# Attention scores in 64-row tiles with four masked key copies, four rotating PSUM banks, and the values stage moved to the middle of the step

## The chip, the cores and the metric

The kernel runs on one core of a Trainium2 chip. The metric is the device time of one execution in microseconds (us), the median over several runs.

## The reference

x has the shape [16, 64, 64, 64] (images n, rows a, columns b, channels d). Four blocks follow each other, each added to x after a layer normalization:

1. Attention over the 16 images, for each pixel (a, b) by itself: q, k, v and a gate from 64 channels, 8 heads of 16 channels, softmax over the 16 images, o times the gate, then a projection back to 64 channels.
2. A mixture of experts on each pixel: router logits for 8 experts, the best two by softmax, a 64 x 64 expert each.
3. An expansion to 128 channels; a running average along the row axis a of the gating half, its sigmoid times the other half, and a contraction to 64 channels.
4. A selection: for each of 32 slots and each image a softmax over the 4096 pixels, the 8 best pixels pooled, a small network, and the result added back to those pixels.

```python
att = jnp.einsum('iabhc,jabhc->ijabh', q, k) * (1.0 / np.sqrt(C))
att = jax.nn.softmax(att, axis=1)
o = jnp.einsum('ijabh,jabhc->iabhc', att, v) * g
```

## The kernel before

The work of blocks 1 to 3 is cut into 128 items, each half a column of the images: 512 tokens in 4 tiles of 128 (32 rows a by 16 images). A software pipeline works on up to nine items at a time. One **slot** is a pass through the body `step(i, q)` on each engine, q being 0 or 1; an operation with lag L works in slot n on item n - L (the table `LAG`: att_t, q, k, gate and v have lag 1, scores 2, values and att_out 3, route and y0 to y3 4, conv_t and expand 5, scan_out 7, pick_t and pick 8). Buffers that live from one lag to another come in pairs. Each engine's order is written out by hand in `step`, the five engines meet through counting semaphores, and `at(i, q, lag)` is the count that stands for "the item with this lag in this slot". Block 4 follows after all slots, in a phase of its own.

TensorE order before: att_t (transposes), scores, q, values, ffn_t, v, scan_out, gate, k, att_out, pick_t, route, pick, conv_t, y0, expand, y1, y2, y3. The first slots and the last ones leave out the parts whose item doesn't exist.

**Scores.** The 8 heads lie along 128 partitions, 16 to a head. To keep heads apart, ScalarE writes 8 copies of k (lines 470 to 474), each with all rows but those of one head set to zero. 32 matmuls in tiles of 128 rows by 32 columns (line 640), 128 columns streamed each, fill one PSUM bank. VectorE takes the maxima (817) and subtracts them (819), ScalarE takes the exponential (507), VectorE sums (852), takes the reciprocal (854) and multiplies by an odd/even head mask to own_den (857); GpSimd forms probs (414), and VectorE transposes them in 32 x 32 blocks to probsT (918). One slot later the values (line 658: 64 matmuls of 32 x 32 tiles) fill the four o_bank banks, and VectorE multiplies them by the gate (839, output ogT; "the gated read" below). Each fp32 matmul appears as two instructions in the trace.

**The gate.** gT is one of the buffers in a pair. ScalarE writes it with a Tanh, at lag 1, and first waits until the gated read of the item that had this buffer, lag 3 in the same slot, is over:

```python
act.wait_ge(filled["gate"], at(i, q, 1))
wait(act, s_og, at(i, q, 3))
s.activation(gT[z1][:], bk("gate")[:], ACT.Tanh, bias=bg_col[:],
             scale=0.5).then_inc(drained["gate"], 1)
```

**PSUM.** Two `shared` banks are used in turn by the operations of `TURNS`; `s_bank` has two banks and `o_bank` four, and six further operations borrow banks of these (`BORROWED`). Before TensorE fills a bank it waits until its last user there is drained, that is, read by ScalarE or VectorE.

ScalarE order before: zT, rounding of ffn, qT, rounding of att, tT, the copy of v, exp, the Tanh of gT, masked copies 0 and 1, rounding of conv, lT (the drain of pick_t), copies 2 and 3, picks, cT, lge, copies 4 and 5, four parts of expand, copy 6, gT plus one, in slots with q = 0 the Tanh of the scan (ema_t), copy 7. VectorE order before: statistics of att, expert sum `mixed` (811), maxima and subtraction of the scores, x2 and statistics of conv, gated read, x3 add (848), sums to own_den, scan gating in slots with q = 1, x1 add (868) and statistics of ffn, statistics of pick, the route's logits (880) and the choice of two experts, yg of y0 and y1 (912), transpose of probs, in slots with q = 0 the scan, yg of y2 and y3 (932), and the gating for q = 0. SyncE issues three groups of eight DMAs a slot: the next x, the normalized x3 and x3.

Of the kernel before, what the change touches and what calls it, by code (L numbers as in the profile page):

```python
# [45 lines left out]
def build(nc, x, ln_w, ln_b, Wq, Wk, Wv, Wg, bg, Wo, bo, router_w, router_b, expert_w, expert_b,  # L46
# [24 lines left out]
    with ExitStack() as ctx:  # L71
# [12 lines left out]
        shared = [ctx.enter_context(nc.psum_tensor(f"shared{i}", [P, 512], F32)) for i in range(2)]  # L84
        s_bank = ctx.enter_context(nc.psum_tensor("s_bank", [P, 2, 512], F32))
# [3 lines left out]
        with ExitStack() as cols:  # L89
# [12 lines left out]
            b_k = cb("b_k", [P, H])  # L102
# [19 lines left out]
            odd_even = cb("odd_even", [P, 2])  # L122
            decay = cb("decay", [P, 8, A])
# [18 lines left out]
            kT = cb("kT", [P, H, QTOK])  # L142
# [26 lines left out]

            filled = {k: sem(f"filled_{k}") for k in TURNS + list(BORROWED)}  # L170
            drained = {k: sem(f"drained_{k}") for k in TURNS + list(BORROWED)}
# [12 lines left out]
            s_sums, s_v = sem("exp_summed"), sem("values_biased")  # L184
# [7 lines left out]
            N_DVE_SETUP = 11  # L192
# [32 lines left out]
            def bank_of(q, name):  # L225
                if name in BORROWED:
                    whose, bank = BORROWED[name]
                    return {"o": o_bank, "s": s_bank}[whose][:, bank]
                return shared[(len(TURNS) * q + TURNS.index(name)) % 2][:]

            def last_drained(i, q, name):

                pos = len(TURNS) * q + TURNS.index(name)
                for back in range(pos - 2, pos - 6 * len(TURNS), -2):
                    slots_back, turn = divmod(back, len(TURNS))
                    prev = TURNS[turn]
                    if not isinstance(i, int) or 0 <= 2 * i + slots_back - LAG[prev] < HALVES:
                        return drained[prev], at(i, slots_back, LAG[prev])
# [96 lines left out]
            def _(pool):  # L335
# [54 lines left out]
                def step(i, q):  # L390
# [9 lines left out]
                    if runs(i, q, 5):  # L400
                        normalize("conv", x2[par(q, 5)], 1.0, 1e-6, i, q, 5, "conv_t")
                    if runs(i, q, 1):
# [5 lines left out]
                    if runs(i, q, 5):  # L408
                        second_part("conv", i, q, 5)
                    if runs(i, q, 2):  # L410

                        pool.wait_ge(s_rden, at(i, q, 2))
                        wait(pool, s_probsT, at(i, q, 3))
                        g.tensor_tensor(probs[:], weights[:].unsqueeze(2).broadcast_to([P, 32, 2, 16]),  # L414
                                        own_den[:].unsqueeze(3).broadcast_to([P, 32, 2, 16]), ALU.mult).then_inc(s_probs, 1)
# [22 lines left out]
            def _(act):  # L438
# [27 lines left out]
                def step(i, q):  # L466
# [33 lines left out]
                    if runs(i, q, 1):  # L500
                        act.wait_ge(filled["v"], at(i, q, 1))

                        wait(act, s_o, at(i, q, 3))
                        s.copy(v_sb[z1][:].rearrange("p t c -> p (t c)"), bk("v")[:]).then_inc(drained["v"], 1)  # L504
# [3 lines left out]
                    if runs(i, q, 1):  # L508
# [8 lines left out]
                        masked_keys(range(0, 2))  # L517
# [7 lines left out]
                    if runs(i, q, 1):  # L525
                        masked_keys(range(2, 4))
# [15 lines left out]
                    if runs(i, q, 1):  # L542
                        masked_keys(range(4, 6))
# [13 lines left out]
                    if runs(i, q, 1):  # L557
                        masked_keys(range(6, 7))

# [5 lines left out]
                    if runs(i, q, 1):  # L565
                        masked_keys(range(7, H)).then_inc(drained["k"], 1)

# [620 lines left out]
```

## Time and profile before

| | before |
|---|---|
| median of 3 runs | 3134.15 us (3130.02 to 3141.3) |
| the profiled execution | 3123.18 us, span 3121.5 us |
| TensorE matmul busy | 2647.5 us (85%) |
| VectorE busy | 2551.6 us (82%) |
| GpSimd busy | 2161.0 us (69%) |
| ScalarE busy | 2005.1 us (64%) |
| mean granted TensorE clock | 0.839 |

The span runs from the first to the last instruction of the profiled execution. Busy shares are means over the span, of which the last 270 us or so belong to block 4. PE is TensorE, PEld its weight loads, DVE VectorE, ACT ScalarE, POOL GpSimd, SP SyncE. A granted clock of 1.00 is 2.4 GHz and one of 0.50 is 1.2 GHz.

### The profile page before, as it was taken

The page shows a single profiled execution, that of the slowest core. Times are in us where ns is not written, and L with a number is a line of the kernel's source. Part 1 is how long each engine was busy: PE and PEld are TensorE (multiplying, and loading weights), DVE is VectorE, ACT ScalarE, POOL GpSimd, SP SyncE. Part 2 cuts the span into 40 slices and gives each one's busy share as a digit, 9 for nine tenths or more (in the row PEclk, how much of TensorE's full clock was granted, in tenths as well). Part 3 has the DMA queues.
Part 4 walks back from the last instruction along what each step waited for, and adds up shares of the span by engine and source line. Part 5 has one row for each costly group of instructions (what it writes and reads, how often), then busy time and mean ns, then how long its engine had stood idle before and what let it go on. Part 6 is the DMA issues. An engine that isn't in the chain of part 4 may idle for free. (4 is left out here: it accounts for less than half of the span.)

```text
span 3121.5 us, 108500 instructions
## 1 busy us (share of the span) xinstructions
PE 2647.5 (85%) x37071; PEld 1969.9 (63%) x37071; DVE 2551.6 (82%) x9002; ACT 2005.1 (64%) x3590; POOL 2161.0 (69%) x2963
## 2 busy tenths in 40 slices
PE   2898898888888888898898898888988988896697
PEld 2666666666666656666666666666666666664586
DVE  2788889888888898888888888888889888885604
ACT  2666767766676676776776766677667676762600
POOL 2677777877777777777787877778777777863000
PEclk9788988887888888888887987889889788885858
DMA  0011101111011010110101111011010010101828
GB/s 17 9 20 18 19 17 19 19 18 19 17 19 18 18 19 17 19 19 18 19 17 18 19 18 19 17 19 19 18 19 18 17 19 18 19 15 19 269 96 337
DMA packets 263153, 106.67 MB, mean 34 GB/s; under 512 B 250257, under 2 KB 254900, under 8 KB 258997
## 3 DMA queue, kind: packets, MB, share of 16 engines
q1 hardware_dynamic: 260933, 93.16, 12.9%
q10 hardware_dynamic: 2160, 12.68, 1.0%
q8 instruction: 40, 0.66, 0.1%
q14 instruction: 20, 0.16, 0.0%
HBM read 55.31 MB, written 50.33 MB: 34 GB/s over the span
## 5 line engine op out<-in xcount | busy, mean ns | idle before, releaser
L472 ACT ACTIVATE kT<-s_bank,b_k,block_of 128x512 f32<-128x512 f32 x1024 | 748.8, 771 | 3.6 <-PE s_bank L609 0.3
L640 PE MATMUL s_bank<-kT,qT 128*32 128x128 f32 x8192 | 396.1, 372 | 187.3 <-issue 187.3
L640 PEld LDWEIGHTS s_bank<-kT,qT 128*32 128x32 f32 x8192 | 349.5, 152 | 226.8 <-issue 224.7
L489 ACT ACTIVATE qT<-shared,b_qkg 128x256 f32<-128x256 f32 x256 | 107.5, 471 | 412.0 <-PE shared L609 412.0
L811 DVE TENSOR_REDUCE mixed<-yg 128x256 f32<-128x2048 f32 x128 | 288.5, 2254 | 0.2
L687 PEld LDWEIGHTS o_bank<-w_o,ogT 128*128 128x128 f32 x2048 | 247.9, 193 | 23.7 <-DVE ogT L839 14.8
L414 POOL TENSOR_TENSOR probs<-weights,own_den 128x1024 f32<-128x1024 f32 x128 | 252.7, 1975 | 1.8 <-DVE own_den L857 1.8
L687 PE MATMUL o_bank<-w_o,ogT 128*128 128x64 f32 x2048 | 246.9, 274 | 4.3 <-DVE ogT L839 3.9
L387 POOL TENSOR_TENSOR split_ffn<-norm_ffn,split_ffn 128x256 fp32r<-128x256 f32 x128 | 93.6, 731 | 215.1 <-ACT split_ffn L464 215.1
L658 PEld LDWEIGHTS o_bank<-probsT,v_sb 32*32 32x32 f32 x16384 | 170.2, 107 | 63.7 <-issue 58.1
L658 PE MATMUL o_bank<-probsT,v_sb 32*32 32x64 f32 x16384 | 196.5, 234 | 1.5 <-DVE yg L932 1.5
L387 POOL TENSOR_TENSOR split_att<-norm_att,split_att 128x256 fp32r<-128x256 f32 x128 | 94.0, 735 | 147.4 <-ACT split_att L464 147.4
L622 PE MATMUL shared<-bias,ones 3*128 3x512 bf16 x256 | 109.3, 427 | 98.3 <-ACT picks L532 52.2
L555 ACT ACTIVATE gpre<-shared,bgate_col 64x256 f32<-64x256 f32 x256 | 181.4, 709 | 13.3 <-PE shared L721 10.3
L593 PE MATMUL shared<-ident,split_att 128*128 128x128 f32 x512 | 111.6, 357 | 69.3 <-ACT prim L555 47.9
L377 POOL TENSOR_TENSOR rstd_ffn<-rstd_ffn,minus_half 128x4 f32<-128x4 f32 x128 | 160.1, 1251 | 10.7
L406 POOL TENSOR_TENSOR v_sb<-v_sb,bv_rows 128x512 f32<-128x512 f32 x128 | 163.1, 1274 | 3.0 <-ACT v_sb L504 3.0
L839 DVE TENSOR_TENSOR ogT<-o_bank,gT 128x512 f32<-128x512 f32 x256 | 163.2, 679 | 1.5 <-PE o_bank L658 1.2
L918 DVE STREAM_TRANSPOSE probsT<-probs 128x1024 f32<-128x1024 f32 x128 | 157.9, 1234 | 2.0 <-POOL probs L414 2.0
L593 PEld LDWEIGHTS shared<-ident,split_att 128*128 128x128 f32 x512 | 78.4, 182 | 123.3 <-issue 68.2
L800 DVE SCALAR_TENSOR_TENSOR gated<-ema_t,prim 64x256 f32<-64x256 f32 x256 | 150.3, 587 | 6.8 <-ACT ema_t L564 1.1
L677 PE MATMUL shared<-w_con,gated 128*128 128x64 f32 x1024 | 141.8, 283 | 7.9 <-DVE gated L800 5.8
(204 smaller groups left out, 7648.6 us busy)
## 6 DMA issues: line engine op xcount, KB each, us to landing
x_in<-in_x SPq DMA_DIRECT2D x1024, 16.0 KB, 1.7
x_scratch<-x SPq DMA_DIRECT2D x1024, 16.0 KB, 1.4
normalized_x_scratch<-norm_pick SPq DMA_DIRECT2D x1024, 16.0 KB, 1.5
xa<-normalized_x_scratch SPq DMA_DIRECT2D x16, 1024.0 KB, 8.1
xb<-x_scratch ACTq DMA_DIRECT2D x8, 1024.0 KB, 10.3
out_x<-xa SPq DMA_DIRECT2D x16, 512.0 KB, 5.3
out_x<-xb SPq DMA_DIRECT2D x16, 512.0 KB, 6.9
xa<-x_scratch SPq DMA_DIRECT2D x4, 1024.0 KB, 6.5
```

Source lines behind the costliest of these rows:

```text
L377: ch.link(g.tensor_tensor(r[:, 1, :], r[:, 0, :], minus_half[:], ALU.pow))
L387: g.tensor_tensor(split[kind][z][:, :, 1, :], norm[kind][z][:], split[kind][z][:, :, 0, :].bitcast(F32), ALU.subtract).then_inc(s_split[ki ...
L406: g.tensor_tensor(v_sb[z][:], v_sb[z][:], bv_rows[:].unsqueeze(1).broadcast_to([P, QT, HC]), ALU.add).then_inc(s_v, 1)
L414: g.tensor_tensor(probs[:], weights[:].unsqueeze(2).broadcast_to([P, 32, 2, 16]), own_den[:].unsqueeze(3).broadcast_to([P, 32, 2, 16]), AL ...
L472: ins = s.activation(kT[:, h, :], bk("k")[:], ACT.Identity, bias=b_k[:, h:h + 1], scale=block_of[:, h:h + 1])
L555: ins = s.activation(dst, src, ACT.Identity, bias=bias[r0:r0 + D], scale=scale)
L593: ins = t_.transpose(bank_of(q, name)[:, t * P:(t + 1) * P], split[kind][par(q, lag)][:, t].rearrange("p k d -> p (k d)").bitcast(F32), id ...
L640: ins = t_.matmul(s_bank[g * 32:(g + 1) * 32, 0, t * P:(t + 1) * P], qT[z][:, c, tok:tok + 32], kT[:, :, tok + c * N:tok + (c + 1) * N], s ...
L658: ins = t_.matmul(o_bank[k * 32:(k + 1) * 32, g, t * 64:(t + 1) * 64], v_sb[z][g * 32:(g + 1) * 32, t, k * 32:(k + 1) * 32], pT[g * 32:(g ...
L687: ins = t_.matmul(bk("att_out")[:, t * D:(t + 1) * D], ogT[:, h, tile(t)], w_o2[:, h, :], start=(h == 0), stop=(h == 1))
L811: v.tensor_reduce(mixed[:], yg[:], AX.X, ALU.add).then_inc(s_mixed, 1)
L839: ins = v.tensor_tensor(by_group(ogT[:, h, :]), o, by_group(gT[z][:]), ALU.mult)
```

## The change

- **Scores.** Head m and head m + 4 share one masked copy of k (`quarter` has ones on both), so four copies are written instead of eight. Each score matmul is split in two, on rows 0 to 63 and 64 to 127 (index u), with 64 streamed columns each; the halves go to banks 0 and 1 of `o_bank`: 64 matmuls instead of 32. VectorE reads both banks. The head order in weights, probs and probsT changes with it.
- **PSUM.** `s_bank` and `BORROWED` go. There are four `shared` banks, and the table `BANK` gives each of 17 operations its bank. `o_bank` is used by scores and values in turn, so scores wait for the last gated read, and values wait for the subtraction of this slot's scores.
- **TensorE order.** Values move from behind q to behind pick_t; v moves from behind ffn_t to behind the values; pick_t is now ahead of both; att_out moves from behind k to behind expand. v has bank 3 after pick_t, route bank 0 after scan_out.
- **VectorE order.** The gated read moves behind x3, the sums, the reciprocal, the gating for q = 1 and the statistics of pick. The x1 add and the statistics of ffn move behind yg of y0 and y1.
- **ScalarE order.** The copy of v moves behind lT; the masked copies are 0 after the Tanh of gT, 1 after the copy of v, 2 and 3 after lge. No copy is left behind ema_t.
- **GpSimd.** own_den is computed here, ahead of probs, and the addition of v's bias comes after both.

```diff
-TURNS = ["att_t", "q", "ffn_t", "v", "scan_out", "gate", "pick", "conv_t", "y0", "expand", "y3"]
-BORROWED = {"y2": ("o", 0), "att_out": ("o", 1), "pick_t": ("o", 2), "route": ("o", 3),
-            "y1": ("s", 0), "k": ("s", 1)}
+TURNS = ["att_t", "q", "ffn_t", "scan_out", "gate", "k", "pick_t", "v", "route", "pick", "conv_t", "y0", "expand",
+         "att_out", "y1", "y2", "y3"]
+BANK = {"att_t": 0, "q": 1, "ffn_t": 2, "v": 3, "scan_out": 0, "gate": 1, "k": 2, "pick_t": 3, "route": 0, "pick": 1,
+        "conv_t": 3, "y0": 1, "expand": 3, "att_out": 0, "y1": 1, "y2": 2, "y3": 3}
...
 # GpSimd
+                    if runs(i, q, 5):
+                        second_part("conv", i, q, 5)
+                    if runs(i, q, 2):
+                        pool.wait_ge(s_rden, at(i, q, 2))
+                        g.tensor_tensor(own_den[:], ssum[:].unsqueeze(2).broadcast_to([P, 32, 2]),
+                                        odd_even[:].unsqueeze(1).broadcast_to([P, 32, 2]), ALU.mult).then_inc(s_own, 1)
+                        pool.wait_ge(s_own, at(i, q, 2))
...
 # ScalarE
-                                               scale=block_of[:, h:h + 1])
+                                               scale=quarter[:, h:h + 1])
...
-                        masked_keys(range(0, 2))
+                        masked_keys(range(0, 1))
...
+                        act.wait_ge(filled["v"], at(i, q, 1))
+                        wait(act, s_o, at(i, q, 3))
+                        s.copy(v_sb[z1][:].rearrange("p t c -> p (t c)"), bk("v")[:]).then_inc(drained["v"], 1)
+                    if runs(i, q, 1):
+                        masked_keys(range(1, 2))
...
-                        masked_keys(range(4, 6))
+                        masked_keys(range(2, 4)).then_inc(drained["k"], 1)
...
 # TensorE
-                        wait_apart(pe, (drained["k"], at(i, q, 2)), (drained["q"], at(i, q, 2)), (s_sub, at(i, q, 3)),
-                                   (drained["y1"], at(i, q, 5)))
+                        wait_apart(pe, (drained["k"], at(i, q, 2)), (drained["q"], at(i, q, 2)), (s_og, at(i, q, 4)))
                         for t in range(QT):
                             for c in range(2):
                                 for g in range(4):
-                                    tok = t * P + g * 32
-                                    ins = t_.matmul(s_bank[g * 32:(g + 1) * 32, 0, t * P:(t + 1) * P],
-                                                    qT[z][:, c, tok:tok + 32], kT[:, :, tok + c * N:tok + (c + 1) * N],
-                                                    start=(c == 0), stop=(c == 1), tile_position=(0, g * 32))
+                                    for u in range(2):
+                                        tok, rows = t * P + g * 32, slice(u * D, (u + 1) * D)
+                                        ins = t_.matmul(o_bank[g * 32:(g + 1) * 32, u, t * D:(t + 1) * D],
+                                                        qT[z][rows, c, tok:tok + 32],
+                                                        kT[rows, :, tok + c * N:tok + (c + 1) * N],
+                                                        start=(c == 0), stop=(c == 1), tile_position=(u * D, g * 32))
...
-                        wait_apart(pe, (s_norm["pick"], at(i, q, 8)))
+                        wait_apart(pe, (s_norm["pick"], at(i, q, 8)), last_drained(i, q, "pick_t"))
...
+                    if runs(i, q, 3):
+                        z = par(q, 3)
+                        wait_apart(pe, (s_probsT, at(i, q, 3)), (s_v, at(i, q, 3)), (s_og, at(i, q, 4)),
+                                   (s_sub, at(i, q, 2) if runs(i, q, 2) else HALVES))
...
+                    if runs(i, q, 1):
+                        bank_free(pe, i, q, "v")
...
+                        bank_free(pe, i, q, "route")
...
 # VectorE
+                    if runs(i, q, 2):
+                        dve.wait_ge(s_exp, at(i, q, 2))
+                        v.tensor_reduce(ssum[:], weights[:], AX.X, ALU.add).then_inc(s_sums, 1)
+                        dve.wait_ge(s_sums, at(i, q, 2))
+                        v.reciprocal(ssum[:], ssum[:]).then_inc(s_rden, 1)
+                    if q == 1 and runs(i, 1, 6):
+                        gate_primary()
+                    if runs(i, q, 7):
+                        dve.wait_ge(drained["scan_out"], at(i, q, 7))
+                        stats("pick", x3[par(q, 7)], i, q, 7)
                     if runs(i, q, 3):
                         z = par(q, 3)
                         dve.wait_ge(s_o, at(i, q, 3))
```

## Rows read from the trace of the kernel before

**Rows 1.** Line 811 by source: duration min/median/max, first and last start.

```profile
L811 DVE TENSOR_REDUCE mixed<-yg x128: 2249/2253/2286, 110.2 to 2852.3; 128x256 f32<-128x2048 f32 x128
```

**Rows 2.** One stretch: PE, PEld, DVE, ACT, POOL busy, PEclk, DMA share, GB/s.

```profile
300.00:2700.00 2400.00, 2110.23 (x30639) 1542.85 (x30638) 2120.67 (x7714) 1687.34 (x3053) 1871.42 (x2553) 0.86 0.10 18
```

**Rows 3.** The waits: who waited for whom, us in total, times, longest.

```profile
PE s_bank L640 <- issue: 187.3, 116, 5.2
...
DVE x L848 <- PE shared L677: 71.1, 88, 2.1
...
DVE smax L817 <- PE s_bank L640: 61.4, 53, 3.9
...
DVE x L868 <- PE o_bank L687: 33.0, 66, 3.1
DVE yg L912 <- PE s_bank L624: 32.8, 31, 1.7
...
ACT gT L512 <- DVE ogT L839: 22.8, 25, 2.0
```

**Rows 4.** The costliest groups on the page: the masked key copies.

```profile
L472 ACT ACTIVATE kT<-s_bank,b_k,block_of 128x512 f32<-128x512 f32 x1024 | 748.8, 771 | 3.6 <-PE s_bank L609 0.3
```

**Rows 5.** Timeline, scores and values of three slots: start, us, what.

```profile
59.48 3.64 PE L640 MATMUL s_bank<-kT,qT 128*32 128x128 f32 x64 [5.17 <-issue]
...
1519.11 1.47 PE L658 MATMUL o_bank<-probsT,v_sb 32*32 32x64 f32 x128
...
1558.04 1.95 PE L640 MATMUL s_bank<-kT,qT 128*32 128x128 f32 x64 [1.47 <-issue]
```

**Rows 6.** Timeline, VectorE from one slot to the next.

```profile
1501.89 0.42 DVE L848 TENSOR_TENSOR x<-shared,x_bc 128x256 f32<-128x256 f32 x1 [1.00 <-PE shared L677]
...
1503.33 0.49 DVE L857 TENSOR_TENSOR own_den<-ssum,odd_even 128x64 f32<-128x64 f32 x1
...
1506.07 0.57 DVE L777 BATCH_NORM_STATS2 bn_pick<-x 128x6 f32<-128x64 f32 x4
...
1519.32 0.69 DVE L819 TENSOR_TENSOR weights<-s_bank,smax 128x512 f32<-128x512 f32 x1
...
1521.43 1.29 DVE L839 TENSOR_TENSOR ogT<-o_bank,gT 128x512 f32<-128x512 f32 x2
```

**Rows 7.** Timeline, ScalarE and VectorE in the middle of a slot.

```profile
1502.22 0.69 ACT L512 ACTIVATE gT<-shared,bg_col 128x512 f32<-128x512 f32 x1 [0.29 <-PE shared L609]
...
1504.13 0.41 ACT L464 CAST split_conv<-norm_conv 128x256 fp32r<-128x256 f32 x1
...
1504.86 0.58 ACT L524 COPY lT<-o_bank 64x512 f32<-64x512 f32 x1 [0.31 <-PE o_bank L694]
...
1507.03 0.16 DVE L880 TENSOR_TENSOR lg<-o_bank,rb_rows 128x32 f32<-128x32 f32 x1
...
1509.62 0.69 DVE L912 TENSOR_TENSOR yg<-shared,gates 128x512 f32<-128x512 f32 x1
```

**Rows 8.** Timeline, TensorE: v, att_out, route, y0's start, y1's end.

```profile
1521.01 1.06 PE L670 MATMUL shared<-w_scaled,zT 128*128 128x128 f32 x8
...
1523.85 1.89 PE L687 MATMUL o_bank<-w_o,ogT 128*128 128x64 f32 x16
...
1526.02 0.96 PE L700 MATMUL o_bank<-w_router,tT 128*128 128x8 f32 x8
...
1528.63 0.38 PE L622 MATMUL shared<-bias,ones 3*128 3x512 bf16 x1 [0.44 <-ACT picks L532]
...
1530.73 0.40 PE L624 MATMUL s_bank<-w_expert_lo,tT 128*128 128x512 f32 x1
```

**Rows 9.** Timeline, TensorE near the start of the run: v twice.

```profile
48.45 2.08 PE L670 MATMUL shared<-w_scaled,zT 128*128 128x128 f32 x8 [0.93 <-ACT qT L489]
...
65.17 1.16 PE L670 MATMUL shared<-w_scaled,zT 128*128 128x128 f32 x8 [0.93 <-ACT qT L489]
```

More of the change, by code:

```diff
@@ L83, in build @@
         picks = sb("picks", [P, NG, TOK])
[L84 to L85 removed]
+        shared = [ctx.enter_context(nc.psum_tensor(f"shared{i}", [P, 512], F32)) for i in range(4)]
         o_bank = ctx.enter_context(nc.psum_tensor("o_bank", [P, 4, 512], F32))
@@ L682, in step @@
                         project("k", 1)
-                    if runs(i, q, 3):
-                        pe.wait_ge(s_og, at(i, q, 3))
-                        for t in range(QT):
-                            for h in range(2):
-                                ins = t_.matmul(bk("att_out")[:, t * D:(t + 1) * D], ogT[:, h, tile(t)], w_o2[:, h, :],
-                                                start=(h == 0), stop=(h == 1))
-                        ins.then_inc(filled["att_out"], 1)
                     if runs(i, q, 8):
-                        wait_apart(pe, (s_norm["pick"], at(i, q, 8)))
+                        wait_apart(pe, (s_norm["pick"], at(i, q, 8)), last_drained(i, q, "pick_t"))
                         for t in range(QT):
@@ L721, in step @@
                         t_.matmul(bk("expand")[:], w_expand_lo[:], cT[:], start=False, stop=True).then_inc(filled["expand"], 1)
+                    if runs(i, q, 3):
+                        bank_free(pe, i, q, "att_out")
+                        pe.wait_ge(s_og, at(i, q, 3))
+                        for t in range(QT):
+                            for h in range(2):
+                                ins = t_.matmul(bk("att_out")[:, t * D:(t + 1) * D], ogT[:, h, tile(t)], w_o2[:, h, :],
+                                                start=(h == 0), stop=(h == 1))
+                        ins.then_inc(filled["att_out"], 1)
                     if runs(i, q, 4):
@@ L829, in step @@
                         stats("conv", x2[z], i, q, 5)
+                    if runs(i, q, 7):
+                        z = par(q, 7)
+                        dve.wait_ge(filled["scan_out"], at(i, q, 7))
+                        dve.wait_ge(s_x2bc, at(i, q, 7))
+                        wait(dve, s_x3_store[z], (column(i, q, 9) + 1) * 128)
+                        wait(dve, s_norm["pick"], at(i, q, 9))
+                        v.tensor_tensor(x3[z][:], tok(bk("scan_out")), x2_bc[z][:], ALU.add).then_inc(drained["scan_out"], 1)
+                    if runs(i, q, 2):
[5 more added lines that the diff above has]
+                        gate_primary()
+                    if runs(i, q, 7):
+                        dve.wait_ge(drained["scan_out"], at(i, q, 7))
+                        stats("pick", x3[par(q, 7)], i, q, 7)
                     if runs(i, q, 3):
@@ L913, in step @@
                                             gates[:, t, :].unsqueeze(1).broadcast_to([P, D, NE]), ALU.mult).then_inc(drained[y], 1)
+                    if runs(i, q, 3):
+                        z = par(q, 3)
+                        dve.wait_ge(filled["att_out"], at(i, q, 3))
+                        dve.wait_ge(s_bo, at(i, q, 3))
+                        wait(dve, s_norm["ffn"], at(i, q, 5))
+                        wait(dve, s_x2, at(i, q, 5))
+                        v.tensor_tensor(x1[z][:], tok(bk("att_out")), x_bo[z][:], ALU.add).then_inc(drained["att_out"], 1)
+                        dve.wait_ge(drained["att_out"], at(i, q, 3))
+                        stats("ffn", x1[z], i, q, 3)
                     if runs(i, q, 2):
@@ L937, in _ @@
                 slots(dve, step)
-        banks = [s[:] for s in shared] + [s_bank[:, k] for k in range(2)] + [o_bank[:, k] for k in range(4)]
+        banks = [s[:] for s in shared] + [o_bank[:, k] for k in range(4)]
         with ExitStack() as imgs:
```

126 lines of the change are left out of this document (37 added, 89 removed).

## The prediction

> **What bounds the kernel now.** I read the views in this order: the page, for busy shares; the stretches of time, for one steady window; one line with its first and last start, for the length of a slot; the waits; then the timeline of two neighbouring slots. The chain that ended last is no help: it covers only the closing phase, which the change leaves alone.
>
> The line that sums the experts runs once a slot, 128 times, from 110.2 to 2852.3 us [rows 1], so a slot is 2742.1 / 127 = 21.59 us. In the window 300 to 2700 us [rows 2] that makes per slot: VectorE busy 2120.67 / 2400 x 21.59 = 19.1 us, TensorE 19.0, GpSimd 16.8, ScalarE 15.2. VectorE is idle 2.5 us a slot. The waits [rows 3] put 71.1 + 61.4 + 33.0 + 32.8 = 198.3 us of that, 1.55 us a slot, down to TensorE results; the other 0.95 us are joins between its own dependent instructions and small waits. TensorE's largest single stall is 187.3 us in front of the scores [rows 3], 1.5 us a slot: it waits there through registers, so the row says "issue", and in every second slot ScalarE's last masked copy, queued behind the Tanh of the scan, is what arrives late. So no engine is saturated; VectorE and TensorE are both within 2.6 us of the slot, and the rest is order. What the change does to the order therefore decides.
>
> **The parts that look like gains.** (a) Four masked copies instead of eight: the copy takes 0.77 us [rows 4], so 3.1 us of ScalarE a slot go, and none stands behind the Tanh of the scan any more; the 1.5 us stall before the scores can go. (b) The scores: 64 instructions of 128 columns took 1.95 us at the full clock and 3.64 at half [rows 5]. After, 128 instructions of 64 columns. Bounds: the values stage already issues 128 instructions of 64 columns in 1.47 us [rows 5], and no less; no overlap of the two row halves leaves today's 1.95 to 3.64. I take the values' price, it is the same count and width: 0.5 to 2 us less TensorE. The Trainium skill ("TensorEngine Tiling (Array Packing)", Theoretical Speedup) allows up to 2x for a contraction of 64; by that the full clock stage would be about 1.0 us, an estimate that no row here shows. (c) The product with the odd/even mask, 0.49 us in the slot shown [rows 6], leaves VectorE. On GpSimd I bound it between 0.2 us and its cost on VectorE twice over, 1.0; I take 0.3. GpSimd has 4.8 us free a slot and its product is read only at the transpose, some 9 us later in the new order, so it is hidden; without that cover it would cost its own time. (d) The reads of the scores from two banks have as many elements as before: nothing. The setup gains one tiny reduction before the loop: nothing. No DMA is added; the three groups of eight on SyncE keep their order and wait for events that merely move.
>
> VectorE's own floor becomes 19.1 - 0.5 + 0.95 = 19.5 us a slot.
>
> **The part that costs.** Follow one wait that the change does not touch. ScalarE's Tanh of the gate (line 512) writes a buffer that the gated read (line 839) of the same slot still needs, two slots' work being in flight in a pair of buffers, and so waits for that read. Today the read comes early: it ended at 1522.7 [rows 6], and the Tanh still waited for it 25 times, 22.8 us in all [rows 3]. The change moves the values behind the scores' reading, and on VectorE the gated read behind the x3 add, the sums, the reciprocal and the statistics of pick. In the slot shown 2.7 us passed from the end of the subtraction (1520.01) to the end of the gated read (1522.72) [rows 6]; now x3 to reciprocal (1501.89 to 1503.33, 1.44 us) and the statistics (1506.07 to 1507.03, 0.96) [rows 6, 7] come in between: 5.1 us, 6 where a slot has the scan's gating there too.
>
> Queued behind the waiting Tanh on ScalarE are the first masked copy, the rounding of conv, the copy lT and then the copy of v. TensorE's v now sits in bank 3 behind pick_t, so it needs lT; and route, which VectorE needs next, is queued behind v. VectorE, having ended the gated read, goes straight to the route's logits. So it waits for a chain that starts only when it finishes:
>
> 1. ScalarE, Tanh start to end of the conv rounding: 1502.22 to 1504.54 = 2.32 us with two masked copies [rows 7], one less 0.77 [rows 4] = 1.55; lT 0.58 [rows 7]; with handoffs 2.2 us.
> 2. TensorE, v 1.06 and route 0.96 [rows 8]: 2.0 us at full clock. First hole: 4.2 us.
> 3. VectorE then works from the logits to the end of y0's product, 1507.03 to 1510.31 = 3.3 us [rows 7].
> 4. Next it wants y1. TensorE from v's start: v 1.06; from the start of route to the end of y1, with pick, conv_t, y0 and expand between them, 1526.02 to 1531.13 = 5.11; and att_out, now ahead of y1, 1.89 [rows 8]: 8.1 us. Second hole: 8.1 - 2.0 - 3.3 = 2.8 us.
>
> The holes make 2.2 + 8.1 - 3.3 = 7.0 us, none of it beside other VectorE work. The other inputs, followed in the same way (exp, scan_out, the transposed probabilities), come in time, since all engines but VectorE gain slack from the longer slot. Slot at full clock: 19.5 + 7.0 = 26.5 us.
>
> **The clock.** TensorE ends the values 1.5 us after the subtraction and then stands for 5.1 - 1.5 + 2.2 = 5.8 us, in every slot. After an idle stretch of 5.17 us the scores took 3.64 us and v, 5.7 us after the restart, 1.16 again [rows 5, 9], so the 1.2 GHz level stood for most of the first 5 us. The page "TensorE: Matmul & The Clock Gate" (Part 1) of the Trainium skill calls the throttled level the default, which activity releases. By that, and the trace agrees, v starts slow in each slot. At half clock v took 2.08 (+1.0) [rows 9]; route with as many weight loads gets likewise +1.0, and conv_t with half as many +0.5 (an estimate). The chain is then 8.1 + 2.5 = 10.6 and the holes 2.2 + 10.6 - 3.3 = 9.5: a slot of 29.0 us, 7.4 more than now.
>
> **The sum.** The holes need lags 1, 3, 4 and 8 together: slots 8 to 127, 120 of them. The execution profiled took 3123.2 us (span 3121.5 and 1.7 around it). 3123 + 120 x 7.4 = 4011. My step 4 adds durations that overlap by about 0.1 at each seam, 0.3 in all and 36 us over the run, so I take 3980. The median of runs lies 11 us above the profiled one: 3990.
>
> **The rivals.**
> - *Full clock.* The stop doesn't lower the clock, or it recovers at once: 26.5 a slot, 3123 + 120 x 4.9 = 3711. For it: v was fast again within 5.7 us of a restart. Against: such stops now come every slot. 0.2.
> - *Only the first hole.* y1 is there when VectorE asks, and the clock is full: 19.5 + 4.2 = 23.7, 3123 + 120 x 2.1 = 3375. It needs 2.8 us of TensorE work to vanish. 0.1.
> - *Half clock all along.* The rest doubles like v, y0 to y1 from 1528.63 to 1531.13 (2.50) and att_out (1.89) [rows 8]: +4.4, a slot of 33.4, 3123 + 120 x 11.8 = 4539. 0.12.
> - *Faster.* The Tanh isn't held by this slot's gated read (its count being met by the last one's), so the chain runs under VectorE's work, and the stall before the scores and half the copies are saved: 19.5 a slot, 3123 - 128 x 2.1 = 2854. It decides if the Tanh starts at least 4.2 us before the gated read ends. Against it stands the row with 25 waits. 0.07.
> - *No change.* Gain and holes cancel: 21.6 = 19.5 + 2.1, half of the first hole. 0.03.
>
> **How the numbers follow.** The slow-start case has 0.48 and gives the forecast, 3990. Differences under 0.3% (9 us) cannot be told from none. Slower 0.90, same 0.03, faster 0.07. The range from the single first hole to near the all-slow case, 3380 to 4450, leaves about 0.15 outside.
>
> **What would show it.** Right: the Tanh waiting on the gated read in nearly every slot, some 4 us each, 500 us in all; VectorE's logits (line 880 now) waiting on TensorE's route 4 to 6 us a slot and its yg product on y1 about 2.5; TensorE idle 5 to 6 us before v, released by lT; v near 2 us; the scores stage near 1.5 and its stall gone; mean clock under 0.8. Wrong: the Tanh starting before the gated read, or logits without a wait. The forecast fails low if the clock stays up, high if it never recovers.

## The result and the profile after

| | before | after |
|---|---|---|
| median | 3137.73 us (3130.02 to 3146.6, 4 runs) | 4466.19 us (4464.67 to 4555.35, 4 runs) |
| the profiled execution | 3123.18 us | 4555.35 us, span 4553.6 us |
| TensorE matmul busy | 2647.5 us (85%) | 3589.7 us (79%) |
| VectorE busy | 2551.6 us (82%) | 2430.6 us (53%) |
| mean granted TensorE clock | 0.839 | 0.594 |

The ratio is 1.423 (95% interval 1.419 to 1.4272): slower by 1328 us. The forecast was 3990 and its range ended at 4450, so the time lies 16 us above the range. The profiled execution of the changed kernel was its slowest of four, 2% over the median, at a clock of 0.594 where the others had about 0.66; its rows show the pattern, and where a size matters the median is used.

The line of the expert sum by source (columns as in [rows 1]), and a steady stretch (as [rows 2]):

```profile
L802 DVE TENSOR_REDUCE mixed<-yg x128: 2250/2253/2287, 124.4 to 4293.7; 128x256 f32<-128x2048 f32 x128
```

```profile
300.00:4200.00 3900.00, 3143.73 (x39867) 2289.43 (x39870) 2127.65 (x8031) 1477.63 (x2751) 1983.15 (x2815) 0.58 0.07 12
```

A slot is (4293.7 - 124.4) / 127 = 32.83 us here. What lies outside the 127 slots is 4555.35 - 4169.3 = 386 us, so at the median a slot is (4466.19 - 386) / 127 = 32.1 us, against 21.59. In a slot of 32.83 VectorE works 2127.65 / 3900 x 32.83 = 17.9 us and TensorE 26.5: VectorE now stands for 14.9 us a slot, not 2.5. The waits of the changed kernel (columns as in [rows 3]) say for what:

```profile
POOL x_bo L423 <- DVE x L899: 1212.9, 126, 9.8
DVE lg L858 <- PE shared L681: 718.2, 125, 5.9
DVE yg L890 <- PE shared L611: 631.5, 128, 5.1
ACT gT L510 <- DVE ogT L851: 610.4, 126, 5.7
...
PE shared L674 <- ACT lT L522: 455.9, 121, 4.3
...
DVE bn_att L768 <- DMA x_in<-in_x: 248.6, 128, 16.9
...
DVE sel L874 <- ACT lge L544: 108.1, 125, 2.3
DVE ogT L851 <- PE o_bank L666: 98.4, 95, 2.8
```

The wait for the load had this row before:

```profile
DVE bn_att L777 <- DMA x_in<-in_x: 34.0, 11, 14.5
```

The Tanh waited for the gated read 25 times before [rows 3] and now does so in 126 slots, 4.8 us each. Read the VectorE rows as a list of holes, each total over its count: the logits 5.7 us a slot, yg 4.9, the load of the next x 1.9, sel 0.9, the gated read 1.0 where it waits (0.8 over all slots). Together 14.2 of the 14.9 us.

One slot in the timeline, all engines:

```profile
1500.90 3.86 SPq L313 DMA_DIRECT2D x_in<-in_x  x8
...
1503.02 2.05 PE L627 MATMUL o_bank<-kT,qT 64*32 64x64 f32 x128
...
1506.07 0.61 DVE L768 BATCH_NORM_STATS2 bn_att<-x_in 128x6 f32<-128x64 f32 x4 [0.40 <-DMA x_in<-in_x]
...
1516.09 1.29 DVE L851 TENSOR_TENSOR ogT<-o_bank,gT 128x512 f32<-128x512 f32 x2 [0.38 <-PE o_bank L666]
1517.48 0.69 ACT L510 ACTIVATE gT<-shared,bg_col 128x512 f32<-128x512 f32 x1 [4.91 <-DVE ogT L851]
...
1519.65 2.08 PE L674 MATMUL shared<-w_scaled,zT 128*128 128x128 f32 x8 [3.69 <-ACT lT L522]
1519.88 0.29 POOL L407 TENSOR_TENSOR own_den<-ssum,odd_even 128x64 f32<-128x64 f32 x1
...
1521.52 1.71 PE L681 MATMUL shared<-w_router,tT 128*128 128x8 f32 x8
...
1523.27 0.19 DVE L858 TENSOR_TENSOR lg<-shared,rb_rows 128x32 f32<-128x32 f32 x1 [5.89 <-PE shared L681]
...
1527.20 3.51 PE L708 MATMUL shared<-w_o,ogT 128*128 128x64 f32 x16
...
1532.44 0.69 DVE L890 TENSOR_TENSOR yg<-shared,gates 128x512 f32<-128x512 f32 x1 [5.05 <-PE shared L611]
1533.05 0.42 DVE L899 TENSOR_TENSOR x<-shared,x_bo 128x256 f32<-128x256 f32 x1
...
1533.54 0.73 POOL L423 TENSOR_TENSOR x_bo<-x_in,bo_rows 128x256 f32<-128x256 f32 x1 [9.84 <-DVE x L899]
```

From 1516.09 to 1523.27 the reader sees the forecast chain link by link: gated read, Tanh, v behind lT, route, logits. What the forecast did not have starts at the last two rows. The x1 add (L899) is now the end of the chain att_out, y1, yg; x_bo on GpSimd waits for it, the eight loads of the next x are issued after x_bo (in the slot ahead they began at 1500.90 and took 3.86 us to issue), and VectorE wants that x for the next statistics at 1506.07.

And the clock, in stretches of 2 us of the same slot (TensorE busy, then granted clock):

```profile
1516.00:1518.00 2.00, 0.00 (x0) 1.00 0.19 30
...
1520.00:1522.00 2.00, 2.00 (x11) 0.50 0.00 0
...
1528.00:1530.00 2.00, 2.00 (x11) 0.50 0.00 0
...
1534.00:1536.00 2.00, 2.00 (x7) 0.50 0.05 10
```

The granted level is 2.4 GHz (1.00) where TensorE stands, and 1.2 GHz (0.50) through the 16 us of work from v to y3. The forecast had it last about 5. Not every slot is like this one. e3 below takes as long as the changed kernel's median and has the same order on TensorE; its trace has one such stretch at 0.50 as well, with v from 1519.16, and in the next slot, with v from 1552.57, the level comes back after 9 to 10 us of work:

```profile
1554.00:1556.00 2.00, 2.00 (x12) 0.50 0.16 25
...
1562.00:1564.00 2.00, 2.00 (x12) 1.00 0.00 0
```

### The profile page after: what moved, and what is told of

It is laid out like the page before. It is cut to its first block and busy times, and to the rows that moved or that the text cites. A ratio compares the mean times of both kernels' runs of the same rounds, so it can differ in the third digit from the quotient of the medians.

```text
span 4553.6 us, 124326 instructions
## 1 busy us (share of the span) xinstructions
PE 3589.7 (79%) x45263; PEld 2650.8 (58%) x45263; DVE 2430.6 (53%) x8875; ACT 1673.3 (37%) x3078; POOL 2170.3 (48%) x3091
## 5 line engine op out<-in xcount | busy, mean ns | idle before, releaser
L674 PE MATMUL shared<-w_scaled,zT 128*128 128x128 f32 x1024 | 263.5, 438 | 455.9 <-ACT lT L522 455.9
L674 PEld LDWEIGHTS shared<-w_scaled,zT 128*128 128x128 f32 x1024 | 226.6, 326 | 479.1 <-ACT lT L522 478.0
L708 PEld LDWEIGHTS shared<-w_o,ogT 128*128 128x128 f32 x2048 | 462.8, 330 | 25.3 <-issue 1.0
L708 PE MATMUL shared<-w_o,ogT 128*128 128x64 f32 x2048 | 445.3, 411 | 0.7 <-DVE ogT L851 0.7
L610 PE MATMUL shared<-w_expert_hi,tT 128*128 128x512 f32 x512 | 403.8, 789 | 0.0
L475 ACT ACTIVATE kT<-shared,b_k,quarter 128x512 f32<-128x512 f32 x512 | 383.1, 776 | 0.2 <-PE shared L603 0.2
L602 PE MATMUL shared<-zT,w_qkg_hi 128*128 128x512 f32 x384 | 285.9, 745 | 60.3 <-ACT tT L502 51.9
L611 PE MATMUL shared<-w_expert_lo,tT 128*128 128x512 f32 x512 | 319.0, 623 | 0.0
L627 PE MATMUL o_bank<-kT,qT 64*32 64x64 f32 x16384 | 257.7, 305 | 4.6 <-issue 4.6
L627 PEld LDWEIGHTS o_bank<-kT,qT 64*32 64x32 f32 x16384 | 229.5, 142 | 46.9 <-issue 46.9
```

The lines of the kernel that those rows point to most:

```text
L602: t_.matmul(bk(name)[:], w_qkg_hi[:, w, :], zT[z1][:], start=True, stop=False)
L610: t_.matmul(bk(y)[:], tT[z4][:, tile(t)], w_expert_hi[:], start=False, stop=False)
L611: t_.matmul(bk(y)[:], tT[z4][:, tile(t)], w_expert_lo[:], start=False, stop=True).then_inc(filled[y], 1)
L627: ins = t_.matmul(o_bank[g * 32:(g + 1) * 32, u, t * D:(t + 1) * D], qT[z][rows, c, tok:tok + 32], kT[rows, :, tok + c * N:tok + (c + 1) * N],
L674: ins = t_.matmul(bk("v")[:, tile(t)], zT[z1][:, tile(t)].bitcast(F32), w_scaled[:, 3, :])
L708: ins = t_.matmul(bk("att_out")[:, t * D:(t + 1) * D], ogT[:, h, tile(t)], w_o2[:, h, :], start=(h == 0), stop=(h == 1))
```

## The experiments

Each starts from the changed kernel unless the diff says otherwise. The ratio is against the kernel before on the same chip; slots are from the first and last start of the expert sum, over 127, in the profiled execution.

**e1, the Tanh freed.** It writes a buffer of its own; the step that adds one, later in the slot, waits for the gated read instead.

```diff
-    wait(act, s_og, at(i, q, 3))
-    s.activation(gT[z1][:], bk("gate")[:], ACT.Tanh, ...)
+    wait(act, s_gp1, at(i, q, 2))
+    s.activation(g_raw[:], bk("gate")[:], ACT.Tanh, ...)
...
-    s.activation(gT[z1][:], gT[z1][:], ACT.Identity, bias=one_col[:])
+    wait(act, s_og, at(i, q, 3))
+    s.activation(gT[z1][:], g_raw[:], ACT.Identity, bias=one_col[:])
```

> The changed kernel with one wait moved: the Tanh of the gate writes a buffer of its own, and the late add of one, which now carries the wait for the gated read, writes the pair buffer. Same instructions otherwise. Theory (order): the chain from the gated read over Tanh, masked copy, rounding, lT, v and route to the logits is what fills the slot; with the Tanh free it runs under VectorE's work, the wait of the logits falls from 5.9 us a slot to about nothing, TensorE no longer stands before v, the clock rises over 0.8, and the slot goes from 32 us to 22 to 24: 3150 to 3400 us. Rival (clock or tiles): the 64-row score tiles or the four banks keep TensorE slow by themselves; then the clock stays near 0.6 and the time above 3900 us.

Measured 3634.56 us (1.1523, 1.147 to 1.1575), slot 25.65. This gives back 832 of the 1328 us, more than any other single edit, and part of that is the clock, which rises from about 0.66 to 0.75. It still ends 235 us above the theory's band. VectorE's longest waits:

```profile
DVE yg L892 <- PE shared L613: 271.3, 128, 5.1
DVE bn_att L770 <- DMA x_in<-in_x: 243.3, 128, 17.2
DVE lg L860 <- PE shared L683: 172.0, 124, 3.0
```

The wait for x_in is as long as with the Tanh held: it has another cause.

**e2, the stand filled.** The Tanh stays held; TensorE multiplies constants, which nobody reads, before v.

```diff
+    bank_free(pe, i, q, "route")
+    for _ in range(16):
+        t_.matmul(bk("route")[:], w_expand_hi[:], w_expert_hi[:], start=True, stop=True)
```

> The changed kernel with 16 matmuls of 512 columns (weights times weights, result never read) put in TensorE's stand between values and v, in the bank that route overwrites. No work is left out. They take 3.4 us at full clock and 6.8 at half, within the stand of about 6 us. Theory: the lasting half clock comes from this stand and from the other one, and it doubles the chain; with it filled the clock rises over 0.8 and the slot goes to the full-clock sum of 26.5 us, 3700 us in all. Rival: the clock has little to do with it, or stays low for another reason; then 4466 us or more.

Measured 3911.08 (1.2461, 1.2426 to 1.2495), clock 0.843, slot 27.69. More work makes it 555 us shorter, though not down to the 3700 expected. att_out takes 1.89 us, its price at full clock:

```profile
1513.62 1.89 PE L711 MATMUL shared<-w_o,ogT 128*128 128x64 f32 x16
```

VectorE's longest waits, to be held against the forecast's slot at full clock:

```profile
DVE lg L861 <- PE shared L684: 541.3, 126, 5.2
DVE bn_att L771 <- DMA x_in<-in_x: 245.9, 128, 21.8
DVE yg L893 <- PE shared L611: 174.1, 128, 5.1
```

The logits wait 4.3 us (worked out: 4.2), yg 1.4 (2.8), and 1.9 for the load (none).

**e3, the gated read ahead of the x3 add on VectorE.**

> The changed kernel with only VectorE's order changed: the gated read goes back ahead of the x3 add, the values stay where the change put them. Theory: the chain starts earlier by the x3 add, the sums, the reciprocal, the gating and the statistics of pick (2.4 us, 3.3 in odd slots), which VectorE then does while the chain runs, so the holes shrink by up to 2.4 to 3.3 us a slot, less if VectorE waits for the values: 4050 to 4300 us. Rival (only the bank order matters): no change, 4466 us.

Measured 4467.66 (1.4231): no change, against the theory. VectorE's holes only move:

```profile
DVE yg L890 <- PE shared L611: 557.6, 128, 5.1
DVE ogT L832 <- PE o_bank L666: 432.4, 128, 6.7
DVE lg L858 <- PE shared L681: 388.5, 125, 3.7
```

The read waits for the values themselves, which stand behind pick_t in mid step. The time is the rival's, but its reason, the order of the banks, is not what the rows show. In the changed kernel VectorE's place for the read was therefore not what made it late; no run puts the values back at their old place.

**e4, the scores alone**: the kernel before with 64-row tiles and four copies, all else in its old order; k waits for the last subtraction, since the scores now fill both banks of `s_bank`.

> The kernel before with only the 64-row score tiles and the four masked copies; bank of scores half 1 is the one that k fills later, so k waits for the subtraction too. Order untouched. Theory: the score stage goes from 1.95 to 3.6 us to about 1.5 to 2, the stall of 1.5 us a slot ahead of it mostly goes, ScalarE loses 3.1 us a slot; the slot goes from 21.6 to about 20 to 20.5 us: 2900 to 3000 us. Rival: the tiles cost the clock or the two halves do not overlap; then 3130 us or more.

Measured 3098.56 (0.9879, 0.9851 to 0.9907): a gain of 38 us, smaller than expected; whether the tiles or the fewer copies give it was not separated. Two score stages in its timeline, at half and at full clock:

```profile
1500.42 2.06 PE L639 MATMUL s_bank<-kT,qT 64*32 64x64 f32 x128
...
1519.33 1.49 PE L639 MATMUL s_bank<-kT,qT 64*32 64x64 f32 x128
```

against 3.64 and 1.95 [rows 5]. The tiles do what the forecast said; VectorE, busy 2185.53 of 2400 us in this kernel, leaves little to gain.

**e5 and e6, att_out early**: between v and route, with the x1 add and the statistics of ffn ahead of the logits (route shares att_out's bank and so waits for the x1 add); e6 frees the Tanh too, as e1.

```diff
-         "pick_t", "v", "route", "pick", "conv_t", "y0", "expand", "att_out", "y1", ...
+         "pick_t", "v", "att_out", "route", "pick", "conv_t", "y0", "expand", "y1", ...
```

> The changed kernel with att_out moved back towards its old place: on TensorE between v and route (bank 0, so route waits for the x1 add), on VectorE the x1 add and the statistics of ffn ahead of the logits. The Tanh's wait stays. Theory (two chains): besides the chain over the Tanh there is a second, from the late att_out over the x1 add, x_bo, the normalization of pick and the next slot's normalization of ffn on GpSimd to ffn_t, scan_out, k and so the values; the two are nearly tied, so that undoing one alone gives some, 150 to 600 us: 3850 to 4300. Rival (Tanh chain alone bounds): that chain gets longer by att_out's 1.9 to 3.5 us ahead of route, though the second hole goes with it: 4400 us or more.

Measured 4240.39 (1.3484, 1.3426 to 1.3542), slot 30.37, within the expected band: 226 us come back. The wait for x_in falls from 248.6 to 37.5 us in all; x1's own wait for att_out, 935.5, takes the place of those on the logits and on yg.

> Both undone: att_out early as in the run before, and the Tanh writes a buffer of its own so that only the late add of one waits for the gated read. Theory (two chains, nothing else large): near the kernel before, slot of 20.5 to 23 us, 3000 to 3300 us, clock over 0.8. Rival (the four-bank table or the values' place hold it up by themselves): over 3450 us, with waits of TensorE on a bank's drain or of VectorE on the values on top of the list.

Measured 3726.01 (1.1851, 1.1788 to 1.1914), slower than e1: a miss. With the Tanh free, att_out in front of route and x1 in front of the logits make VectorE wait 453.4 us in all for att_out, more than the load's wait that goes.

**e7, e1 with x_bo last on GpSimd.**

> The kernel with the staged Tanh (3635 us) and one GpSimd instruction moved: the x_bo add, which waits for the x1 add and so for att_out, goes from ahead of the normalization of pick to the end of the step. att_out stays late. Theory: GpSimd's standing before x_bo (731 us there) pushes the normalizations of pick and ffn and with them ffn_t; with the add last, normalization of pick and x2_bc run during that stand, 3.4 us of GpSimd work leave the second chain: 3250 to 3500 us. Rival (that stand is harmless, the clock or the bank order sets the time): 3600 us or more.

Measured 4046.26 (1.2857), 412 us slower than e1, where a gain was expected. The load's wait stays (252.1 us in all, 243.3 in e1), and those for y1 (552.8) and for the logits (318) about double, at a clock of 0.63 where e1 had 0.75. Moving x_bo behind the rest of GpSimd's work does not make the load come earlier; by which path it costs 412 us was not followed.

**e8 and e12, more on top of e4**: own_den on GpSimd (e8), and the freed Tanh as well (e12).

> The kernel before with the 64-row score tiles and four copies, and also the product with the odd/even mask on GpSimd right before probs. Theory: 0.5 us a slot less on VectorE, which is the busiest engine there (91% in the steady part), 0.3 more on GpSimd, which has slack: 3030 to 3080 us against 3099 without. Rival: VectorE is not the bound; no change, 3090 to 3110.

> The kernel before with the score tiles, four copies, the mask product on GpSimd (3094 us) and the staged Tanh. There the Tanh waits for the gated read 130 us in 72 slots. Theory: that wait goes, ScalarE gains up to 1 us in those slots, of which some reaches the end: 3050 to 3090 us. Rival: ScalarE is off the path there, no change within 0.3%.

Measured 3093.53 (0.9851, 0.9804 to 0.9898) and 3110.02 (0.9896, 0.987 to 0.9922). The mask product's move is worth no more than can be measured, and freeing the Tanh is worth nothing in the old order, where the gated read is early. Both missed what was expected; e8 fits its rival, no change, and e12 lies 0.5% above e8, their intervals overlapping. e8 is the fastest of all kernels run, 5 us ahead of e4.

**e9 and e10, v and route off lT**: v behind ffn_t, route behind the values, pick_t after route, ScalarE's copy of v ahead of lT; Tanh held (e9) and freed (e10).

> The changed kernel with v and route taken out of the way of lT: v goes back to its old place behind ffn_t (bank 3), route stands right behind the values, pick_t behind route; on ScalarE the copy of v goes ahead of lT. The Tanh's wait and the late att_out stay. Theory (v behind lT links ScalarE's late chain to TensorE): the logits no longer wait, TensorE's stand before v goes; the Tanh still holds picks, cT and lge, so VectorE waits for lge instead, 3 to 4 us, and the second hole stays: 3800 to 4200 us. Rival (the Tanh alone sets the time, wherever v stands): 4350 us or more.

> The same and the Tanh in a buffer of its own. Theory: the loop from the expert sum over the statistics of conv, its normalization on GpSimd, its rounding, lT, v, route to y3 is cut as well, since v no longer waits for lT; what stays late is att_out: 3150 to 3450 us with a clock over 0.8. Rival (that loop matters only through the Tanh): no better than the 3635 us of the staged Tanh alone.

Measured 4255.76 (1.3556) and 3687.65 (1.1738); both missed, e9 between its two bands and e10 on its rival's side, 53 us above e1. In e9 the hole at the logits is gone and stands one step on:

```profile
DVE sel L874 <- ACT lge L544: 613.9, 128, 5.2
```

lge, too, is queued on ScalarE behind the Tanh, lT and the picks. TensorE's order was one of several ways for that wait to reach VectorE.

**e11, e1 with filling ahead of ffn_t and v** (10 and 8 products).

> The kernel with the staged Tanh (3635 us, clock 0.75) and matmuls that nobody reads in TensorE's two stands: 8 of 512 columns between values and v, 10 ahead of ffn_t. No work is left out. Theory: what is left there is largely the half clock on a chain that TensorE's part of, v to y3; with both stands filled the clock is over 0.9 and the time 3200 to 3400 us, although 3.8 us of TensorE work are added a slot. Rival (order alone): the added work costs and nothing comes back, 3635 us or more.

Measured 3615.97 (1.1508), clock 0.91, 19 us under e1 and inside the spread of e1's own times: a miss. Filling the stands was worth 555 us with the Tanh held and, net of the work it adds, next to nothing with it free. VectorE's waits for the load (251.8), the logits (248.8) and yg (219.5) remain, 5.7 us a slot.

**e13, e14 and e17, the orders mended together.** e13: v and route as in e9, att_out behind route, x1 ahead of the first yg, Tanh free. e14: the same, Tanh held. e17: e13 with att_out behind conv_t.

> The changed kernel with three orders mended together: the Tanh writes a buffer of its own (as in e1), v and route are off the copy lT (v behind ffn_t, route behind the values), and att_out stands behind route, with x1 and its statistics ahead of the first product of yg. Theory (held Tanh, v behind lT and late att_out are all of the loss): the three holes of e11 that are left (load 2.0, logits 2.0, yg 1.7 us a slot) go, the slot falls to 20.3 to 21.5 us as VectorE's 19.4 and one small hole, 2950 to 3150 us. Rival (something else of the change, its banks or the values at mid step, holds VectorE too): a new wait of over 3 us a slot takes their place, 3350 to 3700 us. Between them the theory has a part of the rest and the wait that is left names the other part.

> As e13, but the Tanh waits for the gated read in place, as in the changed kernel. Theory (the held Tanh holds all that stands behind it on ScalarE, the picks and the gate choice too): e9 showed 4.8 us a slot moved from the logits to lge; with att_out early as well, the load and yg holes go, slot 27 to 30 us, 3750 to 4100 us, with the largest wait on lge. Rival (the held Tanh costs only through v): within 200 us of e13.

> As e13 (the Tanh free, v and route off lT, x1 ahead of the first product of yg), but att_out stands behind conv_t and not behind route, so that the transpose of the picks, lT, the picks and lge no longer wait for the logits' read. Theory (e13's 610 us on lge were made by its own order): sel's wait on lge falls under 1 us a slot, and the time to 3100 to 3300 us, as e13 less most of 610; the change's tiles, table of banks and copies then cost nothing. Rival (some wait always takes the place of the one removed, as VectorE's chain has no slack in this kernel's order): another wait of 3 us or more a slot, on x or yg, 3500 to 3750 us.

Measured 3731.41 (1.192), 3788.82 (1.2109) and 3567.73 (1.1429, 1.1368 to 1.149), slots 26.39, 26.82 and 25.03. e13 takes away the load's wait (36.3 us left) and that of the logits, and makes one of its own: att_out shares a PSUM bank with route, so it waits for VectorE's read of the logits, and the picks and lge queue behind it.

```profile
DVE sel L876 <- ACT lge L545: 610.2, 127, 6.5
...
PE shared L684 <- DVE lg L860: 247.7, 127, 3.0
```

e14 is 57 us slower than e13 and fits both of its expectations: with that wait in both kernels it doesn't tell what the held Tanh costs. e17 removes two thirds of it and gains 164 us, not the expected 430: it lies in the rival's band, with several smaller waits of VectorE, none of 3 us, in place of the one removed:

```profile
DVE yg L902 <- PE shared L613: 255.3, 239, 1.9
DVE sel L876 <- ACT lge L545: 214.0, 125, 3.1
DVE x L891 <- PE shared L702: 182.0, 112, 3.8
```

**e15 and e16, one late piece each put into the kernel before.** e15: the gated read just ahead of the x1 add. e16: att_out behind expand, x1 and the statistics of ffn behind the first two yg.

```diff
 # e16, from the kernel before, TensorE (VectorE's x1 moves likewise)
-    att_out      (behind k)
     pick_t, route, pick, conv_t, y0, expand
+    att_out
     y1, y2, y3
```

pick_t and route, whose banks the values had filled, keep att_out's old wait for the gated read.

> The kernel before, with the gated read moved from its place before the softmax subtraction's sums to just ahead of the x1 addition, and nothing else: the Tanh still waits for it in place. Theory (the late read by itself is the cause of the largest piece): the Tanh's wait on the read, 22.8 us in all before, comes to over 2 us a slot and the time rises by 200 to 500 us, to 3340 to 3640. Rival (the late read only hurts together with v behind lT, which the kernel before does not have: there v stands ahead of the picks): 3120 to 3240 us.

Measured 3861.63 (1.2359, 1.2296 to 1.2421): +728 us, more than expected. Its waits:

```profile
ACT gT L512 <- DVE ogT L859: 506.4, 126, 4.9
...
DVE x L868 <- PE o_bank L687: 415.6, 128, 3.8
PE o_bank L687 <- DVE ogT L859: 412.2, 128, 4.3
```

The Tanh waits 4.0 us a slot; TensorE's att_out waits for the read 3.2, and VectorE for att_out 3.2. The logits wait for nothing in this run. So the late read is costly without the rest of the change, but VectorE stands here behind the read and att_out, not behind the Tanh, v and route; what the Tanh's hold adds in this kernel was not separated.

> The kernel before, with att_out moved behind expand and the x1 addition with its statistics behind the first two yg products, and nothing else. Theory (late att_out makes the next load late): VectorE waits for x_in at the statistics of the att norm, 1.5 to 2.5 us a slot, and the time rises by 180 to 350 us, to 3320 to 3490. Rival (the load has cover in the kernel before, since its GpSimd is less late): the wait on x_in stays under 0.3 us a slot and the time within 3120 to 3220.

Measured 3753.07 (1.1987, 1.1942 to 1.2032): +620 us, again more than expected:

```profile
DVE yg L902 <- PE s_bank L624: 510.7, 127, 5.1
DVE bn_att L777 <- DMA x_in<-in_x: 238.0, 127, 14.2
```

The load's wait, 1.9 us, is what the theory said; it had left out att_out's own length in front of y1, and yg waits 4.0. In both kernels the mean clock fell to 0.70.

**e18, both late pieces in the kernel before**, with 128-row tiles, eight copies and the old banks; pick_t and route wait for the gated read, whose banks they borrow.

> The kernel before with the gated read late (e15, +728 us) and att_out with the x1 addition late (e16, +620 us) together, and nothing of the rest: 128-row score tiles, eight copies, two shared banks in turn. Theory (the two late pieces are the change's loss, since they hold each other up: att_out waits for the gated read): 4250 to 4600 us, near the changed kernel's 4466. Rival (they overlap, since both make the same slot's x1 late): 3850 to 4050 us, and then some 400 to 600 us of the change's loss are due to v and route behind lT or to its banks.

Measured 4420.51 (1.414, 1.4068 to 1.4212), within the theory's band, slot 31.64, clock 0.646. The two alone add to 728 + 620 = 1348; together they cost 1300, and the whole change 1328.

```profile
ACT gT L512 <- DVE ogT L863: 680.6, 126, 6.5
...
DVE yg L902 <- PE s_bank L624: 593.0, 128, 5.1
...
DVE lg L870 <- PE o_bank L693: 329.2, 127, 2.7
DVE bn_att L777 <- DMA x_in<-in_x: 239.9, 128, 14.5
```

All four kinds of wait stand in the changed kernel's list too. But the path to the logits differs (here they wait for pick_t and route, held by the read, there for v behind lT), so their share is 2.6 us a slot, not 5.7, and other small waits and VectorE's own work (1928.38 of 3000 us, 20.3 a slot) are larger. That the totals lie 28 us apart is therefore partly chance: e18 shows that two late pieces can cost this much, not that the changed kernel pays it along the same paths.

## Why the prediction was right in direction and short in size

*Right: the Tanh's chain.* The Tanh waits in 126 slots, 610 us in all (said: 500); TensorE stood 3.7 us ahead of v in the slot shown, until lT (said: 5 to 6). The logits wait 5.7 us a slot, where step 1 with v and route at half clock makes 2.2 + 4.0 = 6.2. e1 shows that this hold is the largest piece in the changed kernel. e15 does not bear on it: there the late read costs through att_out.

*Right: the gains and the places named.* Scores 2.05 us at half clock and 1.49 at full (e4), the stall ahead of them gone (4.6 us of it left in the whole run), own_den 0.29 us on GpSimd (said: 0.3). VectorE without its holes is 32.8 - 14.2 = 18.6 us a slot, under the 19.5 of the forecast.

*Failed first: that the other inputs "come in time", and that SyncE's groups of eight "keep their order and wait for events that merely move".* Three inputs did not: the next x (1.9 us a slot), lge (0.9) and the values (0.8). The load is the one with a mechanism that could be followed: att_out was costed as 1.89 us ahead of y1, and not as what sets x1, x_bo and the eight issues of 3.9 us behind it. e16 shows it alone. e5 and e13 remove it by an early x1. In e2, with the work from v on at full clock, a slot is 27.7 where the forecast had 26.5: +1.9 for the load, +0.7 for the values, -1.4 on yg.

*Failed second: "The clock", taken to stay at 1.2 GHz for the first 5 us.* It stayed for all 16 us from v to y3 in the slot shown, and for 9 us and more in e3's. From v to the second yg passed 12.8 us (1519.65 to 1532.44), where the forecast's chain had 10.6; att_out took 3.51 of it, not 1.89: the largest single excess in the second hole, 4.9 us against 3.3. In e3's trace att_out comes to 3.2 us a slot. The forecast had 2.5 us a slot for the clock; e2 against the median's slot, 32.1 - 27.7, makes it 4.4. The rival "half clock all along", given 0.12, was nearer on the clock, though e3's slots are not all slow, and its 4539 came near partly by chance: it had none of the three late inputs and a floor 0.9 too high.

*A third, small: 120 slots.* All 127 were lengthened: (32.1 - 21.59) x 127 = 1335, the measured 1328. As an account of the miss: 3990 + 127 x (1.2 + 1.9) for the late inputs and the clock + 7 x 7.4 for the slots = 4436. With the 36 us that were taken off for seams it is 4472. The 3.1 us are taken from the measured slots, so that the sum closes is no further evidence.

*What stays open.* In the changed kernel the freed Tanh gives 832 us back, the filled stand 555 and the early att_out 226; each was measured alone, and they overlap. In the old kernel the late gated read and the late att_out make a loss of the change's size (e18), the first in part by other paths. With all three orders mended e17 still loses 447 us, a third of the whole. What keeps it at 25.0 us a slot, with three waits of 1.4 to 2.0 us and a clock of 0.70, was not separated: the table of banks, the values in mid step, or its own order of TensorE. No run puts the values back, and none changes the banks alone.

## What to carry to other kernels

When a wait is followed through a software pipeline, follow it once around: the last consumer in the slot (here x1) frees a buffer, whose refill and transfer the next slot's first instruction needs. An operation set later costs its length in front of whatever it now precedes, and the lateness of whatever it releases. Each of the two late pieces, put by itself into the kernel before, cost over 600 us, and the busy shares say only that VectorE stands, not for what. Of the whole change only the 64-row score tiles with four copies, in the old order, were worth keeping, 1.2 to 1.5% (e4, e8).

## What the hardware showed that was not expected

- The 1.2 GHz level held through 16 us of unbroken work in the slot shown, while the stand of TensorE ahead of it had been granted 2.4 GHz; in e3 the level came back after 9 to 10 us of work in one slot and not in 16 us in the slot before. Matmuls that nobody reads, ahead of v, raised the mean clock from 0.66 to 0.84 and shortened the run by 555 us (e2). With the Tanh free, where VectorE's waits of 5.7 us a slot remained at a clock of 0.91, they gave 19 us, inside e1's spread (e11). The Trainium skill ("TensorE: Matmul & The Clock Gate", Part 1) has activity release the throttled level. The release in e3's second slot agrees with that, and the 16 us without one do not; the measurement decides.
- 128 instructions of 64 columns on 64-row tiles took 1.48 us at full clock (e8, one stage), the same as the 32 x 32 tiles of the values [rows 5]: the forecast's price, not the halving of 1.95.
- A VectorE instruction could last as long as the GpSimd one beside it. In e18's timeline:

```profile
1501.49 1.93 POOL L414 TENSOR_TENSOR probs<-weights,own_den 128x1024 f32<-128x1024 f32 x1
1501.70 1.74 DVE L877 COPY top<-top 128x8 f32<-128x8 f32 x1
```

The copy of eight elements took 1.74 us and ended with GpSimd's product (1503.42 and 1503.44); in the changed kernel's slot the same copy took 0.17.
